# Products with W_dt on two row halves of TensorE, the taps' row by transfer, the first four units in one group, and new order tables

## What is computed

```python
xn = _layernorm(x)
# attn part: rms norm, then
xi, z = split(xr @ W_in)                       # 256 channels each
xc = silu(conv(xi, conv_w, 4 taps) + conv_b)   # causal, per channel
dt, Bm, Cm = split(xc @ W_x, [64, 80])         # rank 64, 16 states
dt = softplus(dt @ W_dt + b_dt)                # 64 -> 256 channels
h[t] = exp(dt * A) * h[t-1] + dt * xc * Bm[t]  # scan over 256 steps, for 256 channels x 16 states
y = (sum over states of h * Cm + D_skip * xc) * silu(z)
s = xn + y @ W_out
# ffn part: 8 experts of 128 -> 256 -> 128, the best 2 of each token
g = silu(sum of score * (relu(xn @ W1 + b1) @ W2 + b2))
out = x + s * g
```

## Time and profile before

| | us |
|---|---|
| median of 3 runs | 278.15 |
| lowest and highest | 278.07, 278.86 |
| the profiled execution, its own time | 278.31 |
| its span, first to last instruction | 275.8 |

### The profile page before, as it was taken

How to read it: one execution, slowest core, us unless ns; L and a number is a source line. 1 busy time by engine, 2 the same in 40 slices (tenths; PEclk the granted TensorE clock), 3 DMA queues, 4 the chain that set the end, 5 groups by cost and what they waited for, 6 DMA issues and landing times. The chain is left out here.

```text
span 275.8 us, 4155 instructions
## 1 busy us (share of the span) xinstructions
PE 257.1 (93%) x1227; PEld 134.4 (49%) x1227; DVE 246.8 (89%) x286; ACT 221.0 (80%) x423; POOL 226.7 (82%) x183
## 2 busy tenths in 40 slices
PE   5999599799999999899999999799999999999983
PEld 3544153265546432455555733336646446555542
DVE  5597996784999999999996999979999998999994
ACT  1578876999879968999889968889978977878560
POOL 5509696629999996659999799859998999899895
PEclk9999889999999999999999999799999999999999
DMA  5938980024292750051476700061598500000002
GB/s 169 296 98 189 227 201 6 3 80 89 55 207 52 182 124 0 0 140 34 110 179 144 181 0 2 1 137 33 133 207 203 152 0 0 2 0 0 2 0 76
DMA packets 18628, 25.63 MB, mean 93 GB/s; under 512 B 6456, under 2 KB 11951, under 8 KB 18608
## 3 DMA queue, kind: packets, MB, share of 16 engines
q1 hardware_dynamic: 17986, 24.71, 38.2%
q0 software_dynamic: 192, 0.52, 0.9%
q10 hardware_dynamic: 430, 0.14, 0.2%
HBM read 8.13 MB, written 1.31 MB: 34 GB/s over the span
## 5 line engine op out<-in xcount | busy, mean ns | idle before, releaser
L438 POOL TENSOR_TENSOR hc<-hs,Ct 128x1024 f32<-128x1024 f32 x63 | 148.6, 2376 | 12.0 <-DVE hs L925 7.9
L925 DVE TENSOR_TENSOR_SCAN hs<-dec,pdbu 128x1024 f32<-128x1024 f32 x62 | 139.6, 2275 | 0.0
L618 ACT ACTIVATE dec<-rep,negA 128x512 f32<-128x512 f32 x124 | 84.8, 726 | 0.6 <-DMA rep<-dt_u 0.5
L901 DVE TENSOR_TENSOR pdbu<-rep,px 128x1024 f32<-128x1024 f32 x60 | 71.2, 1219 | 9.8 <-PE px L1150 5.5
L1170 PE MATMUL px<-xnT,w 128*128 128x512 f32 x128 | 66.3, 624 | 1.7 <-ACT dtp L699 0.9
L1176 PEld LDWEIGHTS px<-w,hT 128*128 128x128 f32 x512 | 60.3, 192 | 15.3 <-issue 9.6
L1176 PE MATMUL px<-w,hT 128*128 128x128 f32 x512 | 63.4, 278 | 1.4 <-ACT hT L734 1.2
L560 POOL TENSOR_TENSOR acc<-acc,ysc 128x512 f32<-128x512 f32 x30 | 38.2, 1274 | 14.9 <-ACT ysc L723 9.8
L723 ACT ACTIVATE ysc<-px,score 128x128 f32<-128x128 f32 x120 | 34.3, 368 | 17.4 <-PE px L1176 17.1
L734 ACT ACTIVATE hT<-px,cols 128x512 f32<-128x512 f32 x64 | 43.9, 695 | 4.9 <-PE px L1170 4.7
L1062 PE MATMUL py<-hc,rsel 128*32 128x512 f32 x252 | 35.6, 604 | 0.0
(11 more groups left out here) (157 smaller groups left out, 248.2 us busy)
## 6 DMA issues: line engine op xcount, KB each, us to landing
rep<-dt_u SPq DMA_DIRECT2D x116, 128.0 KB, 2.4
Ct<-bc_rows SPq DMA_DIRECT2D x16, 256.0 KB, 5.2
w<-in_L_ffn_W SPq DMA_DIRECT2D x1, 1024.0 KB
x_sb<-in_L_attn_x SPq DMA_DIRECT2D x1, 768.0 KB, 5.6
out<-xn SPq DMA_DIRECT2D x3, 256.0 KB, 2.7
rep<-dt_u POOLq DMA_DIRECT2D x4, 128.0 KB, 3.7
win<-in_L_attn_W_in SPq DMA_DIRECT2D x1, 256.0 KB, 3.0
bc_rows<-dtp SPq DMA_DIRECT2D x4, 64.0 KB, 1.6
```

The costliest lines, as they stand in the source:

```text
L438: eng.tensor_tensor(hc[:, n % HC_RING], hs[:, n % HS_RING], Ct[:, k % 2, j:j + 1, :].to_broadcast([P, 2, CH]), ALU.mult).then_inc(hc_last ...
L618: act.activation(dec[:, n % DEC_RING, i, :], rep[:, q, 0, :], ACT.Exp, scale=negA[:, q, j:j + 1])\
L901: dve.tensor_tensor(pdbu[:, at:at + 2, :], rep[:, 2 * pair:2 * pair + 2, 1, :], B[:, None, :].to_broadcast([P, 2, CH]), ALU.mult).then_inc ...
L925: dve.tensor_tensor_scan(states.rearrange("p b t -> p (b t)"), dec[:, n % DEC_RING].rearrange("p b t -> p (b t)"), pdbu[:, at:at + 2, :].r ...
```

## The change

1. **Row halves.** `W_dt` is loaded as two tiles of 64 rows, one for each half of the channels, on partitions 0 to 63 and 64 to 127 of `wdt`. ACT copies the result of `dt` twice: to `dtp` as before, and its 64 dt rows once more to `dt_low`, on partitions 64 to 127. `v0` multiplies on rows 0 to 63 and waits for the first copy only, `v1` on rows 64 to 127 and waits for both. The zeroing of the lower half of `wdt` is dropped.
2. **Taps by transfer.** The taps go from memory to all 128 partitions in one transfer (512 KB), issued last of ACT's six. The zeroing, the square of ones and the two products are dropped, and `keep_busy` issues 14 products in their place.
3. **First group.** The first four units are summed in one call at slot 9, in the order 0, 2, 1, 3, once all four are multiplied. Before they were summed two at a time at slots 7 and 11.
4. **Tables.** All orders are written anew, `v0` before `tn` in `PRE_JOBS` among them.

The diff, cut (the new tables of chunks 1 to 3 are left out):

```diff
-PRE_JOBS = ["tr", "xc0", "xc1", "dt", "tn", "v0", "v1", "B0", "e0", "B1", "e1"]
+PRE_JOBS = ["tr", "xc0", "xc1", "dt", "v0", "tn", "v1", "B0", "e0", "B1", "e1"]
 EARLY = {
-    0: ["gl", "z1", "m1a", "m0b", "z0"], 1: ["m1b"], 2: ["m0a"], 10: ["gs"], 14: ["gb"],
+    0: ["gl", "m1b", "m0b", "z1"], 1: ["m0a", "z0"], 2: ["m1a"], 10: ["gs"], 11: ["gb"],
 }
 TABLE = [{
-    1: ["tr"], 3: ["xc0"], 6: ["xc1"], 9: ["z0", "z1"], 11: ["dt"], 13: ["y0", "y1"],
-    14: ["m2a", "m2b", "tn", "v", "gl"], 16: ["m3b"], 18: ["y2", "m3a"], 19: ["m4b"], 20: ["m4a", "y3", "m5a"],
...
+    1: ["tr"], 5: ["xc1"], 7: ["xc0"], 9: ["z0", "z1"], 11: ["dt", "y0"], 13: ["y1", "m2b", "tn"],
+    14: ["m2a", "gl"], 15: ["v"], 16: ["m3b"], 19: ["m3a", "y2", "m4b"], 20: ["m4a"], 21: ["y3"], 22: ["m5a"],
...
+FIRST_SUM = 9
-BUSY = {"row": 3, "tr": 2, "xc1": 2}
+BUSY = {"row": 14, "tr": 2, "xc1": 2}
...
-        wdt = sb("wdt", [P, DIN])
+        wdt = sb("wdt", [DB * RANK, P])
-        b2d = sb("b2d", [TPC * EXPERTS, TPC, D])
+        b2_all = sb("b2_all", [P, TPC, D])
+        b2d = b2_all[0:TPC * EXPERTS]
+        dt_low = b2_all[P - RANK:P, :, :].rearrange("p t d -> p (t d)")
...
-            sp.dma_start(wdt[0:RANK, :], W_dt[:, :]).then_inc(w_proj, 16)
+            for b in range(DB):
+                sp.dma_start(wdt[RANK * b:RANK * (b + 1), :], W_dt[:, b * P:(b + 1) * P]).then_inc(w_proj, 16)
...
-            act.wait_ge(row_zero, 1)
-            act.dma_start(cw_row.rearrange("p a b -> p (a b)"), conv_w.rearrange("d a k -> a (d k)")).then_inc(w_row, 16)
...
+            act.dma_start(hc[:, 0].rearrange("p a b -> p (a b)"),
+                          conv_w.rearrange("d a k -> (a d k)").partition_broadcast(P)).then_inc(w_row, 16)
...
-                    ins = act.activation(dtp[0:RANK + 2 * STATES, :], src[0:RANK + 2 * STATES, :], ACT.Copy)
+                    act.activation(dtp[0:RANK + 2 * STATES, :], src[0:RANK + 2 * STATES, :], ACT.Copy).then_inc(dt_copied, 1)
+                    ins = act.activation(dt_low[:, :], src[0:RANK, :], ACT.Copy)
...
-            dve.memset(hc[:, 0, :, :], 0.0).then_inc(row_zero, 1)
-            dve.memset(wdt[RANK:P, :], 0.0).then_inc(setup, 1)
...
-            dve.wait_ge(cw_spread, 1)
+            dve.wait_ge(w_row, 16)
...
-            pe.wait_ge(w_row, 16)
-            pe.wait_ge(row_set, 1)
-            for h in range(2):
-                last = pe.matmul(pdbu[:, h, :], ones_sq[:, :], hc[:, 0, h, :], start=True, stop=True)
-            last.then_inc(cw_spread, 1)
...
-                for n in (2 * m, 2 * m + 1):
+                for n in (0, 2, 1, 3) if m == 1 else (2 * m, 2 * m + 1):
...
-                    wait_emptied(pe, "dt", k)
+                    pe.wait_ge(dt_copied, k + 1) if job == "v0" else wait_emptied(pe, "dt", k)
-                    pe.wait_ge(setup, N_SETUP)
-                    last = pe.matmul(dst[:, :], wdt[:, b * P:(b + 1) * P], dtp[:, :], start=True, stop=True)
+                    last = pe.matmul(dst[:, :], wdt[RANK * b:RANK * (b + 1), :], (dtp[0:RANK], dt_low)[b],
+                                     start=True, stop=True)
...
-                if (n - LAG) % 4 == 0 and 0 <= (n - LAG) // 4 < UNITS // 2:
+                if n == FIRST_SUM:
+                    reduce(1)
+                elif (n - LAG) % 4 == 0 and 2 <= (n - LAG) // 4 < UNITS // 2:
                     reduce((n - LAG) // 4)
```

More of the change, by code:

```diff
@@ L83 @@
 }, {
-    "gate_y": [22, 34], "last_table": [45],
+    "gate_y": [22, 36], "last_table": [31],
 }]
 START = {
-    "second": [1], "gate": [1, 1, 2, 2, 3, 3, 4, 5, 6, 6, 7, 7, 10], "gate_e": [0], "gate_p": [7], "third": [7],
+    "second": [2], "gate": [1, 2, 3, 3, 4, 4, 4, 4, 5, 7, 7, 7, 7], "gate_e": [1], "gate_p": [8], "third": [10],
 }
-AHEAD = [2, 9, 5, 2, 3, 2, 2, 3, 2, 2, 4, 3, 3, 4, 3, 4, 1, 2, 2, 3, 3, 6, 2, 4, 3, 3, 2, 1, 2, 3, 2, 2]
+AHEAD = [2, 8, 3, 2, 4, 3, 2, 2, 2, 3, 1, 1, 3, 3, 1, 3, 0, 2, 2, 3, 3, 3, 2, 3, 3, 2, 2, 1, 2, 3, 4, 4]
@@ L216, in mamba_moe @@
         hc = sb("hc", [P, HC_RING, 2, CH])
-        cw_row = hc[0:1, 0, :, :]
+        taps = hc[:, 0].rearrange("p a b -> p (a b)").rearrange("p (d k) -> p d k", k=TAPS)
         B_first = hc[:, HC_RING - 1]
@@ L261, in mamba_moe @@
         hc_last = sem("hc_last")
+        dt_copied = sem("dt_copied")
         reduced = sem("reduced")
@@ L267, in mamba_moe @@
         N_REP = 16 * 2 * GROUP
[L268 to L269 removed]
+        N_SETUP, N_SELECTED = 2, QUADS + DB + 1
+        N_ROWS, N_PROJ, N_MOE = 5, 4, 3 + TPC
         xv_dram = x.rearrange("b (h p) d -> p (b h) d", p=P)
@@ L816, in weigh_taps @@
                                       taps[:, b * P:(b + 1) * P, t], ALU.mult).then_inc(tapped, 1)
-            taps = pdbu[:, 0:2, :].rearrange("p a b -> p (a b)").rearrange("p (d k) -> p d k", k=TAPS)
             stats(0)
@@ L1058, in reduce @@
                         continue
-                    pe.wait_ge(hc_done, n + 1)
+                    pe.wait_ge(hc_done, 4 if m == 1 else n + 1)
                     for i in range(2):
@@ L1063, in reduce @@
                                          stop=j == QUADS - 1)
-                last.then_inc(reduced, 1)
+                last.then_inc(reduced, 2 if m == 1 else 1)
             def spread_u(i):
```

28 lines of the change are left out of this document (11 added, 17 removed), and 24 rows, old and new, of the table TABLE.

## The result

| | before | changed |
|---|---|---|
| median of 4 executions, us | 278.5 | 286.3 |
| lowest and highest, us | 278.07, 279.66 | 284.57, 289.40 |
| ratio, 95% interval | | 1.031 [1.024, 1.037] |
| profiled execution: time, span, mean granted clock | 278.31, 275.8, 0.986 | 289.40, 287.3, 0.957 |

The forecast was 275.4 us, the range 272.5 to 279.3; the changed kernel takes 286.3, above it.

A forecast was written before the change was run, and what follows sets the result against it. PE's queue was taken as the bound, setting DVE's pace. Start -0.8, gb into the hole -1.05, two pairs -1.44 and second copy +0.5 summed to -2.8 us, giving 275.4 us; range 272.5 to 279.3.

The forecast's parts named there:

- The bound: Whole kernel: PE's queue sets DVE's pace, so time taken out of it moves all that stands behind it.
- The start, -0.8: Kernel's start: idle products replacing the taps' spreading end at 7.4 to 7.6, so the start comes 0.8 us earlier.
- I take no wait: ACT's use of A_log at the start: no wait despite the taps' transfer; up to 1 us possible.
- First products: First W_dt products: v1 behind tn delays the first decay about 0.6 us, beside the path hanging on v0 alone.
- The first group, -1.05: Before dt of chunk 1: one group call saves nothing by itself, but gb moved into the hole gains 1.05 us.
- costs nothing unless PE came 2 us sooner: First group: waiting for all four products by C costs nothing; POOL ends the fourth at 43.35, PE sums from 45.30.
- The pairs, -1.44: v0 and v1 in chunks 1 to 3: side by side 1.0 us for 1.72; two pairs gain 1.44, the third nothing.
- the rival in which a bank comes late: v0, v1 pairs: both run apart because a bank comes late, giving back 2.2 us; 277.6 us, chance 0.14.
- the rival built on it: v0, v1 pairs: strict program order makes three passes, 0.43 us less gained in each of two; 276.3 us, chance 0.14.
- The second copy, +0.5: ACT's second copy of dt: PE waits 0.5 us more for dt's bank at 117.58; bound 2.0 us.
- The other tables, 0 and 1.5 either way: Remaining new orders: same work in another order, not summed, taken as 0 with 1.5 us held either way.
- The rate, a rival at 0.10: PE's waits: new falls of its rate cost 1.4 to 1.7 us each; three give 280.0 us, slower; chance 0.10.

The follow-up runs named there:

- e3: Kernel before with the row halves alone (second copy of dt, W_dt in two halves): 276.75 us, ratio 0.998 to before.
- e4: Kernel before with the taps by transfer alone: 277.92 us, ratio 1.002 to before.
- e5: Kernel before with the first four units summed in one group at slot 9 alone: 280.21 us, ratio 1.010 to before.
- e10: Changed kernel with idle products in four of PE's waits of chunk 0: 282.89 us, ratio 1.024 to before.
- e7: Changed kernel with the gate's steps of chunk 0 at the slots of before: 286.31 us, no ratio.
- e1: Kernel before with the new order tables alone: 277.41 us, ratio 1.004 to before.
- e15: Changed kernel with full-row W_dt products in chunk 3 and idle products in chunk 0's waits: 281.75 us, ratio 1.016 to before.
- e8: Changed kernel without row halves (W_dt's products on all rows, one copy of dt): 280.38 us, ratio 1.013 to before.
- e9: Changed kernel with W_dt's products of chunk 3 alone on all 128 rows, second copy kept: 282.49 us, ratio 1.020 to before.
- e14: Kernel before with idle products alone, 10 ahead of z0 of chunk 0 and 6 ahead of dt of chunk 1: 274.71 us, ratio 0.991.
- e13: Kernel before with row halves, taps by transfer and A_log's loads early: 277.74 us, ratio 0.999 to before.
- e6: Changed kernel with the first units summed two by two again: 284.47 us, ratio 1.023 to before.
- e11: Kernel before with row halves and idle products ahead of z0 of chunk 0 and dt of chunk 1: 276.85 us, ratio 1.000.

## Why the prediction was wrong

**The bound.** That time taken out of PE's queue moves all behind it was no use as a price. None of the terms of about 1 us reached the end by itself (e3, e4, e5). Where they went is shown in part: the group's into the wait before `dt` (3.55 us for 1.72), the start's into that for `A_log` (1.77 and, in e4, 1.85).

**The start, -0.8.** The idle products end at 7.6, as the step has it (7.4 to 7.6; from 6.9 to 8.2 in other profiles), and the taps are weighed from 8.99, before 9.2. Two things failed. "I take no wait" for `A_log`: it was 1.77 us. And the step took 0.88 us for the weighing; it took 1.52, 0.4 of it with the taps in SBUF even beside an idle GpSimd (1.29 for 0.87) and 0.2 more while GpSimd works. With `A_log` early the first scan came sooner (21.8 for 23.0 in one profile), with some luck at PE's start.

**First products.** `v1` stands behind `tn` as forecast, and the first decay comes 0.8 later (22.33 for 21.50) where the step had 0.6; the first scan too (23.8 for 23.0). The prediction had this "beside" the path, and it was: unit 1's product by B begins at 27.63 for 27.80.

**The first group, -1.05.** The hole before `dt` is 1.94 (forecast up to 2.5; 1.72 before), and sixteen instructions of the group take 1.92 at the full rate (e10), as forecast. The step said that the added wait "costs nothing unless PE came 2 us sooner". PE came 1.2 us sooner (ready at 46.82 - 2.75 = 44.07, before 45.30) and POOL 3.4 later (42.11 + 4.66 = 46.77 for 43.35), since DVE's products and POOL's had collided. In e5, without that collision, PE does not wait at the group, and the wait before `dt` is 3.55 us, as the step had it for a group without `gb` in the hole, but priced at nothing: e5 spends 12.3 us at half rate for 5.4, and by before's line that is all of its loss. The collision was in the rows before (POOL's four products from 33.12 had DVE's products just ahead of them at 31.8 and 33.0), and I did not ask what a gate moved by a slot would do to it. At equal clock the gate's start of before (e7) is worth some 2 us.

**The pairs, -1.44.** Their size was right in the changed kernel, where both banks are free: 1.06 for 1.72 in chunk 1 (1.12 in chunk 2), and the third apart. With the orders of before it is 1.46 (e3, chunk 1) and 1.72, no saving (chunk 2), since the bank of `v1` is emptied 0.4 and 0.6 us after `v0` has begun. That is the rival in which a bank comes late, and one reason why the row halves alone bring so little. That `v1`'s first instruction starts at 68.85 and `v0`'s second at 69.38 speaks against the rule of the Trainium skill ("TensorE: Matmul & The Clock Gate", Part 3) and against the rival built on it, provided that the two passes of a product stand together in the program, which no view shows. But in e3 nothing of the saving reaches the end of the kernel.

**The second copy, +0.5.** 0.62 measured with the old orders (e3), so its size was right; in the changed kernel the new order hides most of it (0.25 in chunk 2).

**The other tables, 0 and 1.5 either way.** Put at nothing without a sum, they cost 1 to 2 us by themselves (e1), at the edge of the bounds or just outside. What they do together with the row halves and the late gate, 2.7 us over before's line in all, no term of the sum covers. The wait for B, 15.3 us for 5.5 in the changed kernel but 6.0 in e1, is not the tables' own doing alone. The timelines where those orders are tight (chunk 0's gate, the wait of 1.90 for `gate_e`) could have been walked; I did not do it.

**The rate, a rival at 0.10.** This is the step that failed: the sum had no term for the rate, that is, it took the time at half rate to stay as it was, and that time went from 5.4 to 21.4 us. The rival was the case. "It decides from two and a half" falls was the right price (1.4 to 1.7 each in the prediction, 1.6 measured) with the wrong number: 21.4 us at half rate for 5.4 is 4.7 stretches more, 7.5 us at 1.6 each. By the fitted lines it is (287.4 - 279.2) - (277.9 - 274.8) = 5.1 us. The prediction counted only waits of PE behind which the rate might fall. It did not count a stretch of 13.65 us in which PE is full.

**The account.** Of 9.5 us (287.4 - 277.9), 5 to 7.5 are time at half rate, 1 to 2 the orders by themselves. The rest, up to 3.4, lies in the mechanisms together with the new orders and is not fully divided: e15 has 3.8 at the clock of before, which takes in the price of its own added products; at equal clock some 2 us go away with the gate's start of before (e7) and as much with the row halves undone (e8, only four executions, from -1.5 to +2.5). Shown by taking it away: the clock (e9, e10, e15), which brought 4.5 to 5.7 us, and in the kernel before e14. Shown by adding it: the cost of the orders by themselves (e1). The sizes at equal clock rest on a line and on few executions.

**Open.** Why half-row products bring the rate down at 184 to 188 in the new order and not in the old one (the profiles of e3 and e13), and why it then can stay down for 10 to 13.65 us. With the new orders and half-row products in chunk 3 all five profiles have a fall there (the two of the changed kernel, e6, e7, e10), for 13.65, 3.41, 10.24, 13.66 and 3.42 us; with full rows none of four has (e1, e8, e9, e15). e9 changed them alone, but for a load of W_dt over 64 more rows and a memset at the start, and the stretch was gone; it does not show how. Why nothing fell near 176 in e14, where nothing was added, is open too.

## What to carry over

Before costing what an edit takes out of a full engine, count the places at which that engine will stand still for long, and price each at what a fall costs in the traces (here 1.6 us; falls followed waits of 1.92, 1.94, 2.75 and 3.55 us, but not each time): a saved microsecond ahead of a wait only makes the wait longer. If the kernel before has such holes, fill them with idle products first: it was worth 0.9% here, more than any of the four edits, though nothing in the kernel with the row halves (e11). And sort the executions by granted clock before comparing two kernels that differ by 1%.
